# GNN layer on one core: the column sums of the first pass taken over four tiles at once

## What is computed

```python
h   = relu(layernorm(x))                          # 12500 x 128
m   = concat(h[src], 0, edge_attr) @ W1 + b1      # 212500 x 256
a   = relu((m - mean(m)) * rsqrt(var(m) + eps) * g1 + be1)   # statistics over all edges
agg = segment_sum(a, dst) / max(count, 1)         # 12500 x 256
h2  = concat(h, 0, agg) @ W2 + b2                 # 12500 x 385
out = x + relu(relu(batchnorm(h2)) @ W3 + b3)     # 12500 x 128
```

## Time and profile before

| | |
|---|---|
| median of 3 runs | 2862.91 us (2860.04 to 2866.8) |
| the profiled execution | 2858.51 us, its span 2856.6 us |
| busy: PE / DVE / ACT / POOL | 2275.7 / 1396.0 / 972.9 / 1765.4 us |
| table stage | 0 to about 111 us |
| first pass (first to last gather) | 110.9 to 2103.7 us |
| second pass | from 2117 us to about 2775 us |
| bytes moved by DMA | 740.85 MB, 259 GB/s on average |

### The profile page before, as it was taken

How to read it: one execution, slowest core, us unless ns; L and a number is a source line. 1 busy time by engine, 2 the same in 40 slices (tenths; PEclk the granted TensorE clock), 3 DMA queues, 4 the chain that set the end, 5 groups by cost and what they waited for, 6 DMA issues and landing times. The chain is left out here.

```text
span 2856.6 us, 34294 instructions
## 1 busy us (share of the span) xinstructions
PE 2275.7 (80%) x12138; PEld 883.5 (31%) x12138; DVE 1396.0 (49%) x2298; ACT 972.9 (34%) x1601; POOL 1765.4 (62%) x1850
## 2 busy tenths in 40 slices
PE   4677767767777778777777877787779999999989
PEld 4322212212222222222222222222234334344449
DVE  6422222353333333333333333333248988898968
ACT  4422222222222222222222222222235556566646
POOL 7777777777777777777777777777742222222210
PEclk9888888879998899889988888889879999999999
DMA  9677777768777777777767777777749999999956
GB/s 284 214 247 245 238 241 246 258 215 283 245 244 240 239 249 245 235 252 238 257 230 242 253 239 241 247 245 243 235 169 339 348 349 336 343 346 347 343 195 170
DMA packets 270622, 740.85 MB, mean 259 GB/s; under 512 B 46391, under 2 KB 98661, under 8 KB 270448
## 3 DMA queue, kind: packets, MB, share of 16 engines
q1 hardware_dynamic: 189152, 525.28, 51.6%
q0 software_dynamic: 78432, 212.46, 24.7%
q10 hardware_dynamic: 2864, 0.86, 0.1%
HBM read 501.63 MB, written 236.81 MB: 258 GB/s over the span
## 5 line engine op out<-in xcount | busy, mean ns | idle before, releaser
L618 POOL DMA_INDIRECT sums<-P_d,late x1581 | 1512.0, 956 | 483.5 <-issue 468.0
L1347 PE MATMUL psum<-late,sums 128*128 128x512 f32 x1660 | 937.6, 690 | 259.9 <-DVE sums L1048 248.4
L1048 DVE TENSOR_TENSOR sums<-psum,sums 128x1024 f32<-128x1024 f32 x396 | 483.8, 1222 | 1317.1 <-DMA sums<-P_d,late 1268.9
L706 ACT ACTIVATE sums<-sums 128x1024 f32<-128x1024 f32 x416 | 438.9, 1055 | 1518.3 <-DVE sums L1048 1510.9
L1347 PEld LDWEIGHTS psum<-late,sums 128*128 128x128 f32 x1660 | 316.6, 212 | 883.3 <-issue 468.4
L1290 PE MATMUL psum<-sums,ones 128*32 128x512 f32 x830 | 495.4, 682 | 6.7 <-ACT sums L706 6.7
L1091 DVE TENSOR_TENSOR late<-late,psum 128x1024 f32<-128x1024 f32 (+1 forms) x407 | 482.2, 1212 | 34.1 <-DMA late<-m_d 32.5
L1291 PE MATMUL psum<-sums,ones 128*32 128x512 f32 x830 | 495.4, 682 | 0.0
L1292 PE MATMUL psum<-sums,ones 128*32 128x512 f32 x830 | 495.3, 682 | 0.0
L1293 PE MATMUL psum<-sums,ones 128*32 128x512 f32 x830 | 495.3, 682 | 0.0
L647 POOL TENSOR_TENSOR late<-dst_f,iota 128x384 f32<-128x384 f32 (+1 forms) x139 | 115.3, 830 | 377.6 <-PE psum L1459 373.5
(11 more groups left out here) (206 smaller groups left out, 1990.9 us busy)
## 6 DMA issues: line engine op xcount, KB each, us to landing
m_d<-sums SPq DMA_DIRECT2D x415, 512.0 KB
late<-m_d SPq DMA_DIRECT2D x406, 512.0 KB, 5.4
sums<-in_ea_main SPq DMA_DIRECT2D x103, 512.0 KB
sums<-P_d,late POOLq DMA_INDIRECT x1581
P_d<-sums SPq DMA_DIRECT2D x24, 512.0 KB, 3.2
nodes<-in_x SPq DMA_DIRECT2D x24, 256.0 KB, 6.6
late<-in_x SPq DMA_DIRECT2D x24, 256.0 KB, 3.2
out<-late SPq DMA_DIRECT2D x24, 256.0 KB, 2.5
```

The lines of the kernel that those rows point to most:

```text
L618: pool.indirect_dma_start(out=m_s[s][0:r, k * L:(k + 1) * L], out_offset=None, in_=P1_d, in_offset=bass.IndirectOffsetOnAxis(ap=idx[0:r, G ...
L706: act.activation(q_s[g % Q_SLOTS][0:r, 0:w], m_s[g % M_SLOTS][0:r, 0:w], ACT.Square).then_inc(s_q, 1)
L1048: dve.tensor_tensor(m_s[s][0:r, 0:w], ps_m[place_m[g]][0:r, 0:w], m_s[s][0:r, 0:w], ALU.add).then_inc(s_m, 1)
L1347: ins = pe.matmul(ps_m[place_m[g]][:, 2 * i * L:2 * (i + 1) * L], ea[:, i * P:(i + 1) * P], W1c[:, :], start=True, stop=g not in xg_no, sk ...
```

## The change

ScalarE makes two passes over each group: a Copy and a Square, both read m with the four tiles of a feature next to each other (a step of 256 columns) and write them packed, so that `turned` holds m and its squares as [feature][tile]. VectorE then adds the four tiles of each feature in one tensor_reduce over 2048 elements with 512 results, and TensorE takes the column sums with a single matmul of 32 x 512, four groups behind. There are two `turned` slots of 2048 columns in place of three `q_s` slots of 1024, and three `tile_sums` of 512 columns, of which two lie in `sums`. AHEAD is 7. The slot of m is free for the next gather after ScalarE's Square (`s_q`), no longer after TensorE's sums.

```diff
-Q_SLOTS = 3
+Q_SLOTS = 2
+TILE_SUMS = 3
+SUMS_BEHIND = 4
-AHEAD = 9
+AHEAD = 7
-        taken = [1024 * (M_SLOTS + Q_SLOTS + EA_SLOTS)]
+        taken = [1024 * (M_SLOTS + 2 * Q_SLOTS + EA_SLOTS) + 2 * GE]
+        turned = [flat[:, 1024 * (M_SLOTS + 2 * i):1024 * (M_SLOTS + 2 * i + 2)].rearrange("p (v f t) -> p v f t", v=2, t=GT)
+                  for i in range(Q_SLOTS)]
+        tile_sums = [flat[:, taken[0] - 2 * GE:taken[0] - GE], flat[:, taken[0] - GE:taken[0]], mid[:, 0:2 * L]]
-            pool.memset(pick[:, :], 0.0).then_inc(s_pick, 1)
-            pool.wait_ge(s_pick, 1)
-            for i in range(4):
-                pool.memset(pick[32 * i:32 * i + 1, i // 2:i // 2 + 1], 1.0 / E).then_inc(s_pick, 1)
+            pool.memset(pick[:, :], 1.0 / E).then_inc(s_pick, 1)
...
                 if g >= M_SLOTS:
                     pool.wait_ge(s_mw[s], 16 * (g // M_SLOTS))
-                    pool.wait_ge(s_st, g - M_SLOTS + 1)
+                    pool.wait_ge(s_q, g - M_SLOTS + 1)
...
                 act.wait_ge(s_m, g + 1)
                 if g >= Q_SLOTS:
-                    act.wait_ge(s_st, g - Q_SLOTS + 1)
-                act.activation(q_s[g % Q_SLOTS][0:r, 0:w], m_s[g % M_SLOTS][0:r, 0:w], ACT.Square).then_inc(s_q, 1)
+                    act.wait_ge(s_sum, g - Q_SLOTS + 1)
+                m = m_s[g % M_SLOTS][0:r, 0:w].rearrange("p (t f) -> p f t", f=L)
+                act.activation(turned[g % Q_SLOTS][0:r, 0, :, 0:tiles(g)], m, ACT.Copy)
+                act.activation(turned[g % Q_SLOTS][0:r, 1, :, 0:tiles(g)], m, ACT.Square).then_inc(s_q, 1)
...
+            def sum_tiles(g):
+                r = rows(g)
+                if g >= TILE_SUMS:
+                    dve.wait_ge(s_st, g - TILE_SUMS + 1)
+                dve.wait_ge(s_q, g + 1)
+                dve.tensor_reduce(tile_sums[g % TILE_SUMS][0:r, :].rearrange("p (v f) -> p v f", v=2),
+                                  turned[g % Q_SLOTS][0:r, :, :, 0:tiles(g)], AX.X, ALU.add).then_inc(s_sum, 1)
...
+                if g:
+                    sum_tiles(g - 1)
...
+            sum_tiles(NG - 1)
...
             dve.wait_ge(s_st, NG)
-            dve.tensor_copy(totals, ps_tot[:, 0:L]).then_inc(s_half, 1)
-            dve.wait_ge(s_half, 1)
-            dve.tensor_tensor(totals, totals, ps_tot[:, L:], ALU.add).then_inc(s_tot, 1)
+            dve.tensor_copy(totals, ps_tot[0:1, :]).then_inc(s_tot, 1)
...
             def stats(g):
-                pe.wait_ge(s_q, g + 1)
...
+                pe.wait_ge(s_sum, g + 1)
+                r = rows(g)
+                pe.matmul(ps_tot[0:32, :], ones[0:r, 0:32], tile_sums[g % TILE_SUMS][0:r, :], start=(g == 0), stop=(g == GF),
+                          skip_group_check=True).then_inc(s_st, 1)
...
-                if g >= 3:
-                    stats(g - 3)
+                if g >= SUMS_BEHIND:
+                    stats(g - SUMS_BEHIND)
...
             for h in range(2):
-                ins = pe.matmul(ps_fin[:, h, :], totals[:, h * P:(h + 1) * P], pick[:, :], start=True, stop=True)
+                for v in range(2):
+                    ins = pe.matmul(ps_fin[:, h, v:v + 1], totals[:, v * L + h * P:v * L + (h + 1) * P], pick[:, :],
+                                    start=True, stop=True)
```

More of the change, by code:

```diff
@@ L160, in build @@
         m_s = [flat[:, 1024 * i:1024 * i + 1024] for i in range(M_SLOTS)]
-        q_s = [flat[:, 1024 * (M_SLOTS + i):1024 * (M_SLOTS + i + 1)] for i in range(Q_SLOTS)]
-        ea_s = [flat[:, 1024 * (M_SLOTS + Q_SLOTS + i):1024 * (M_SLOTS + Q_SLOTS + i + 1)] for i in range(EA_SLOTS)]
+        turned = [flat[:, 1024 * (M_SLOTS + 2 * i):1024 * (M_SLOTS + 2 * i + 2)].rearrange("p (v f t) -> p v f t", v=2, t=GT)
+                  for i in range(Q_SLOTS)]
+        ea_s = [flat[:, 1024 * (M_SLOTS + 2 * Q_SLOTS + i):1024 * (M_SLOTS + 2 * Q_SLOTS + i + 1)] for i in range(EA_SLOTS)]
+        tile_sums = [flat[:, taken[0] - 2 * GE:taken[0] - GE], flat[:, taken[0] - GE:taken[0]], mid[:, 0:2 * L]]
+        assert len(tile_sums) == TILE_SUMS and 2 * L == GE
         assert M_SLOTS >= ROW_SLOTS + 2 and ROW_SLOTS * BN_ <= 2048
@@ L219, in build @@
         fb_hot_lo = late[:, 3 * EW + GE // 2:3 * EW + GE].bitcast(BF16).rearrange("p (k n) -> p k n", k=GT)
-        totals = mid[:, 0:L]
+        totals = mid[0:1, 0:2 * L]
         diag = mid[:, 2 * L:3 * L].rearrange("p (h f) -> p h f", h=2)
@@ L305, in build @@
         t_col = sb("t_col", [P, 2])
-        pick = sb("pick", [P, 2])
+        pick = sb("pick", [1, 1])
         g1_col, be1_col = sb("g1_col", [P, 2]), sb("be1_col", [P, 2])
@@ L362, in build @@
         s_cnt = sem("s_cnt")
+        s_sum = sem("s_sum")
         s_st = sem("s_st")
-        s_pick, s_half, s_tot, s_fin = sem("s_pick"), sem("s_half"), sem("s_tot"), sem("s_fin")
+        s_pick, s_tot, s_fin = sem("s_pick"), sem("s_tot"), sem("s_fin")
         s_eat = sem("s_eat")
@@ L630, in _ @@
             flag = pool.alloc_register("wide_pool")
-            pool.wait_ge(s_pick, 5)
+            pool.wait_ge(s_pick, 1)
             pool.wait_ge(s_m, NG)
@@ L1042, in _ @@
                         dve.wait_ge(s_mw[s], 16 * (g // M_SLOTS))
-                        dve.wait_ge(s_st, g - M_SLOTS + 1)
+                        dve.wait_ge(s_q, g - M_SLOTS + 1)
                     dve.tensor_tensor(m_s[s].rearrange("p (t f) -> p t f", f=L), ps_m[place_m[g]].rearrange("p (t f) -> p t f", f=L),
@@ L1364, in _ @@
                     pe.transpose(psum[0:2 * GC, 7, 0:P], rng[:, :], ident[:, :]).then_inc(s_rngT, 1)
-            stats(NG - 3)
-            stats(NG - 2)
-            stats(NG - 1)
+            for g in range(NG - SUMS_BEHIND, NG):
+                stats(g)
             pe.wait_ge(s_tot, 1)
-            pe.wait_ge(s_pick, 5)
+            pe.wait_ge(s_pick, 1)
             pe.wait_ge(s_m, NG)
             for h in range(2):
-                ins = pe.matmul(ps_fin[:, h, :], totals[:, h * P:(h + 1) * P], pick[:, :], start=True, stop=True)
+                for v in range(2):
+                    ins = pe.matmul(ps_fin[:, h, v:v + 1], totals[:, v * L + h * P:v * L + (h + 1) * P], pick[:, :],
+                                    start=True, stop=True)
             ins.then_inc(s_fin, 1)
```

## The result

The changed kernel takes 2892.55 us (median, 2888.06 to 2896.8) where the kernel before takes 2861.47 on the same chip: a ratio of 1.0109, 95% interval 1.0092 to 1.0127, so about 31 us or 1.1% slower. I had forecast 2881 with a range of 2871 to 2905, slower: the direction and most of the mechanism hold, but 12 us of the 31 were not in my sum. That the result still lies in the range is in part luck: the upper end of the range was kept for a burst on VectorE and for ScalarE or TensorE being late, and none of these came. The profiled execution took 2888.06 us with a span of 2886.1.

A forecast was written before the change was run, and what follows sets the result against it. GpSimd's back-to-back gathers were taken to bound the first pass. Gathers 15.1, between the passes 4.1 and second pass -0.5 summed to +18.7 us, on the median 2862.9 giving 2881.5 us; range 2871 to 2905.

The forecast's parts named there:

- a burst on VectorE: First pass, window work after group 105 with a 2.3 us reduction put in front: adds 0, up to 5 us.
- ScalarE or TensorE being late: Allowance at the range's high end, reaching on to 2905 us, for these engines being late in stretches.
- What bounds the kernel: First pass: GpSimd issues gathers back to back, one every 1.261 us; a group of four costs 5.04 us.
- TensorE's part, 0: First pass: fewer column-sum matmuls save 0, since the four bands run side by side and TensorE isn't waited for.
- The clock rival: First pass: TensorE's granted clock falls and TensorE becomes the pace, +170 us, about 3050 us; chance 6%.
- The gathers, +15.1: Three groups move from table stage into first-pass loop: 12 more gathers at 1.261 us, +15.1 us.
- ScalarE: First pass: two strided passes a group at 2.06 us each instead of one of 1.055; 1754 us of work, not the bound.
- VectorE: First pass: 415 reductions of 2.29 us, 950 us in all; 81% busy, adding 0 to the time.
- Between the passes, +4.1: From last full add through totals to `pick`: longer chain of passes, reductions and counts' end, +4.1 us, bounds 3.3 to 4.9.
- Second pass, -0.5: Two more groups loaded cost 3.1 us, loads going on 3.5 us earlier: net -0.5 us, bounds -3.6 to +3.1.

The follow-up runs named there:

- a_near: The changed kernel with the comparison that builds near reading its second input from PSUM instead of SBUF: 1.0036 of the kernel before, 2865.4 us.
- b_onemm: The kernel before, issuing in groups 1 to 413 only the last of the four matmuls of column sums: ratio 0.9988, 3 us less.
- b17: The kernel before with at most 17 groups that use gathered x rows instead of 20: ratio 1.0062, 2871.7 against 2856.6 us.
- b_near: The kernel before with the comparison that builds near reading its second input from PSUM instead of SBUF: ratio 0.9950, 2841.6 us.
- a_same: The changed kernel run once more, unaltered, on the chip of the others: 1.0110 of the kernel before, 2889.0 us.
- a_contig: The changed kernel with ScalarE's two passes reading m in the order of memory, so the sums mix features: 1.0102 of the kernel before.
- a_tail: The changed kernel with the counts' end put in front of the last two reductions: 1.0107 of the kernel before.
- a_psum: The changed kernel with the counts' tensor_scalar operations reading the row of column numbers from PSUM instead of SBUF: 1.0063 of the kernel before.
- b_ahead7: The kernel before with 7 instead of 9 groups loaded ahead: ratio 1.0004.

## Why the prediction came out as it did

**What bounds the kernel: right.** GpSimd's gathers set the first pass, in all twelve kernels run. Over twice the work on VectorE and over three times that of ScalarE did not move them by itself (a_near); neither did fewer matmuls (b_onemm).

**TensorE's part, 0: right.** Fewer matmuls, the same busy time, and nothing waits for it. The clock rival is out: PEclk 0.86 against 0.87.

**The gathers, +15.1: right.** 1593 of them, 17 groups with x rows, and GpSimd idle for 14.8 us ahead of the pass. b17 has this term alone and measures +0.62%, 14 to 22 us; a_near against b_near gives 15.5 in the traces.

**ScalarE, right in size.** I took 2.06 us a pass, it is 1.99 and 1.98: the row of VectorE's strided read was a good price, 0.9 ns an element over the pass without a step. The 2.4 us worked out from the Trainium skill's Vector Engine (DVE) Microarchitecture Reference, Measured stream behaviour on trn2, were not reached. I had taken the dearest row of its table, 2.5 ns an element for VectorE with a step of 24 words; for steps of 72 words and for jumps of 4 KB the same table has 1.7 to 1.8 ns. Here it is 1.94 ns on ScalarE (1.99 us for 1024), between the two. ScalarE's 1624 us in the pass are below the 1754 I had, because the passes are a little shorter and the records of two passes overlap by 0.1 us. It is no pace maker.

**VectorE, right in size and wrong in effect; here lie 9 to 11 of the 12 us that the sum lacks.** The reductions take 2.28 us (forecast 2.29) and hold no gather: the gathers beside them take 0.95. The step that failed is the premise that a group of four gathers "costs 5.04 us whatever the others do", and that nothing is to be charged for VectorE's work beside GpSimd. I had seen the gather of 1.67 us at 665.18, put it down to L1013 next to it, and took it for a fixed part of the spacing. It was L1005, the comparison just ahead, and its cost depends on where a gather starts in it. In the trace of before it stands there:

```profile
665.09 0.95 DVE L1005 TENSOR_TENSOR late<-dst_f,iota 128x768 bf16<-128x768 f32 x1
```

At the gather's start 0.86 us of it are left; less 0.13 that is 0.73, and the gather is 0.72 longer than usual. Had the places been even, the extra would be 0.27 us a comparison (0.82 squared over twice 1.25) or 19 us in 70. The order of before happens to be kinder: 7 to 13.5 us over 1.2527 in its five traces with that comparison. With the reduction put ahead of the counts it is 19.5 to 22.8 in after, a_same, a_contig and a_tail, but 9.5 in a_psum, where the operations around the comparison are shifted a little too. Beside the comparison alone it is 9 to 12.5 us in the five and 20 to 24 in the four. The change put 2.3 us of reduction ahead of the counts and so came upon the expensive places; that it would be these could not be told from the order alone.
The Trainium skill bears on this: SBUF — State Buffer, Who interferes with whom, says that a VectorE instruction with two SBUF inputs contends with a GpSimd instruction that reads SBUF, and that tensor_reduce never does on this chip. Both agree with these traces, 0.79 us beside L1010 and 0 beside L1048 (some 700 gathers start during a reduction in the changed kernel, with a mean of 947 ns). The same section infers that tensor_tensor should not stall GpSimd's DMAs; for an indirect gather b_near measures the opposite, 0.5% of the kernel.

**Between the passes, +4.1: too small; it is +6.7.** A part of that is my sum: the 4.3 and the 0.5 worked out there make 4.8, and I entered 4.1, the middle of the bounds. The chain was followed rightly up to the last reduction (ends forecast at 2136.6 on the clock of after, seen at 2136.8). The step that failed is that the last sums' matmuls would be done under the counts' end. They take 0.94 us a record, one after another, at a granted clock of 0.50 (from 2126 to 2138 us), the lower of the two clock levels, after stretches in which TensorE waits 2 to 3 us for each reduction. The clock was 0.50 before the change as well (2104 to 2113 us); and the earlier trace rows have the copy waiting 2.42 us for the sums' matmuls, which my chain left out. In the changed kernel the copy of the totals waits 1.5 us for these matmuls after the counts' end. `pick` takes 1.86 us instead of the 1.5 in my sum. That is 4.8 + 1.5 + 0.4, the 6.7 measured. From the last full add to the totals it is 12.0 us, where I had expected 10 to 11.

**Second pass, -0.5: not refuted, and not shown to the microsecond.** The loads go on 3.3 us sooner after the first product, as forecast, and b_ahead7 has no change in time (-1.4 to +3.7 us by its interval). The stretch from the first clip to the end differs by 0.6 us between the two profiled executions, but it scatters between 738 and 749 us over all traces, so that this closeness is chance. Its mean is 741 us in the six traces of kernels without the change and 744 in the seven with it: a loss of a few us there can't be ruled out.

The account for the change is then 15.0 for the gathers, 9 to 11 for their lost time, 6.7 between the passes, 31 to 33 us, against 31 measured. Of the 12 us that my sum lacked, 9 to 11 are the held gathers, 1.9 the last matmuls and `pick`, 0.7 the slip in the sum.

**A version that beats both** is b_near, the kernel before with one operand moved to PSUM: 2841.6 us, 0.50% under it. The change as it stands can't reach that: it pays the three groups and the stretch between the passes in any order (a_near).

## What to carry to other kernels

When one engine's issue sets the pace, count what a change does to the list of its instructions first. Here a slot layout 2048 columns larger cost 12 gathers, which no engine's busy time shows. Then look at that engine's longest instructions and find whose work covers them exactly, by start and end and over all of them, before calling its spacing a constant. Here an operation that came out too long by "what is left of" another one was being held by it, and moving either of them in the order changed the time without a change in the work. Beside several suspects, as here, only an experiment that takes one of them away tells which it was: the first guess, the tensor_scalar operations, was wrong.

## What the runs showed of the hardware

- The comparison, a VectorE tensor_tensor of 128x768 with both inputs in SBUF, holds up an indirect DMA on GpSimd that starts during it, until about 0.13 us before its own end; with one input in PSUM it doesn't. In b_near the 58 gathers that start in the comparison take no extra time; before, 54 took 11.0 us extra. A gather that starts just ahead of the comparison is not held (579 of 581), and the comparison keeps its 0.95 us.
- A tensor_reduce of 2048 elements (2.28 us) does not lengthen the gathers beside it: those that start during one in the changed kernel, some 700, have a mean of 947 ns.
- Four float32 matmuls into four bands of 32 partitions of PSUM take the time of one: TensorE is busy 1501 us in the first pass with four, 1507 with one.
- ScalarE reading with a step of 1 KB needs 1.99 us for 1024 elements, 1.06 without; the write was packed in both.
- Executions of one kernel differ by up to 12 us here (2849.7 to 2862.1), and so do single traces: the length of the second pass from first to last clip lies between 634 and 648 us over all kernels. The 1 to 2 us that my account leaves open lie within that.
